# Attention maxima transposed at the fourth place of a head step instead of the fifth, with the sign and the split into two parts moved behind the transpose

## The reference

```
x = x + Wo(softmax(mask(rope(Q) rope(K)^T / sqrt(32))) V) + bo      # Q, K, V from layernorm(x)
x = x + down(silu(gate(ln(x)) * gs) * (up(ln(x)) * us)) * ds        # 512 -> 1408 -> 512
```

## Time and profile before

| | |
|---|---|
| median of 3 runs | 755.08 us (752.31 to 756.74) |
| profiled execution: time, span | 756.7 us, 754.9 us |
| granted TensorE clock, mean | 0.995 |
| busy share of the span: PE, PEld, DVE, ACT, POOL | 97%, 71%, 59%, 41%, 33% |
| stage B, two consecutive steps | about 18.3 us, 14 such pairs with everything in them |

### The profile page before, as it was taken

How to read it: one execution, slowest core, us unless ns; L and a number is a source line. 1 busy time by engine, 2 the same in 40 slices (tenths; PEclk the granted TensorE clock), 3 DMA queues, 4 the chain that set the end, 5 groups by cost and what they waited for, 6 DMA issues and landing times.

```text
span 754.9 us, 10665 instructions
## 1 busy us (share of the span) xinstructions
PE 732.0 (97%) x3563; PEld 537.5 (71%) x3563; DVE 442.2 (59%) x1103; ACT 308.7 (41%) x641; POOL 246.4 (33%) x224
## 2 busy tenths in 40 slices
PE   7999999979999999999999999999999999999996
PEld 7788888755665655555555547878788888888884
DVE  6979584987777777777777637863243125114113
ACT  3232232256666666666655562223322232222221
POOL 0626251502114142414141436832232223223222
PEclk9999999999999999999999999999999999999998
DMA  8586568635566666666676475650001001001001
GB/s 281 187 280 232 197 251 278 251 127 158 167 168 180 166 177 181 170 180 175 167 194 167 111 208 171 250 227 1 0 3 55 0 1 56 0 0 56 1 1 58
DMA packets 54318, 104.39 MB, mean 138 GB/s; under 512 B 14820, under 2 KB 18404, under 8 KB 53748
## 3 DMA queue, kind: packets, MB, share of 16 engines
q1 hardware_dynamic: 54264, 103.72, 44.7%
HBM read 69.62 MB, written 38.21 MB: 143 GB/s over the span
## 4 chain that ended last, share of the span: by engine, by line
PE 83%; issue 5%; DVE 4%; DMA 3%; ACT 2%; POOL 2%; SPq 0%; DVEq 0%; POOLq 0%; ACTq 0%
PE ps L1101 38%; PE ps L1240 17%; PE ps L1316 9%; PE ps L1219 8%; PE ps L1126 8%; DMA q_st<-neg_max_T 2%; PE ps L1093 2%; POOL hid_lo L592 1%; ACT p L680 1%; ACT o_raw L687 1%; PE ps L1137 1%; PE ps L1160 1%; SPq L421 0%; DMA x_st<-in_x 0%; DVE stats L796 0%
## 5 line engine op out<-in xcount | busy, mean ns | idle before, releaser
L680 ACT ACTIVATE p<-ps 128x384 f32<-128x384 f32 (+3 forms) x384 | 159.5, 489 | 35.0 <-PE ps L1219 34.4
L841 DVE CUSTOM_DVE_ANT_0 masked<-ps,mask_qk 128x512 bf16<-128x512 f32 (+1 forms) x240 | 113.6, 502 | 66.9 <-PE ps L1126 66.0
L1219 PE MATMUL ps<-q_st,k_st 99*128 99x384 f32 (+2 forms) x384 | 135.6, 361 | 4.2 <-ACT p L680 1.3
L1240 PE MATMUL ps<-p,v_slot 128*64 128x512 f32 (+3 forms) x768 | 137.3, 494 | 0.2 <-ACT o_raw L687 0.2
L1052 DVE SCALAR_TENSOR_TENSOR hid<-ps,us_sb,silu 128x512 f32<-128x512 f32 x44 | 33.0, 751 | 165.2 <-PE ps L1101 159.5
L1126 PE MATMUL ps<-k_st,q_st 96*128 96x512 f32 (+2 forms) x384 | 127.8, 355 | 1.0 <-DVE row_max L841 0.9
L592 POOL TENSOR_TENSOR hid_lo<-hid,hid_hi 128x512 fp32r<-128x512 f32 x44 | 56.8, 1292 | 172.2 <-ACT hid_hi L756 172.2
L561 POOL TENSOR_SCALAR_AFFINE_SELECT p<-p 128x512 f32<-128x512 f32 x64 | 40.7, 637 | 202.9 <-ACT p L680 202.8
L1240 PEld LDWEIGHTS ps<-p,v_slot 128*64 128x64 f32 x768 | 50.1, 136 | 74.3 <-issue 62.0
L1126 PEld LDWEIGHTS ps<-k_st,q_st 96*128 96x128 f32 x384 | 72.5, 190 | 26.4 <-issue 17.7
L1219 PEld LDWEIGHTS ps<-q_st,k_st 99*128 99x128 f32 x384 | 72.3, 190 | 18.7 <-ACT p L680 9.6
(11 more groups left out here) (119 smaller groups left out, 1081.9 us busy)
## 6 DMA issues: line engine op xcount, KB each, us to landing
qk_scratch<-st_hi SPq DMA_DIRECT2D x32, 512.0 KB, 3.8
q_st<-qk_scratch SPq DMA_DIRECT2D x32, 384.0 KB, 3.9
k_st<-qk_scratch SPq DMA_DIRECT2D x32, 384.0 KB, 5.0
flag_st<-in_ffn SPq DMA_DIRECT2D x32, 264.0 KB, 2.8
ffn_copy<-in_ffn SPq DMA_DIRECT2D x32, 264.0 KB, 3.2
qk_scratch<-st_lo SPq DMA_DIRECT2D x16, 512.0 KB, 3.8
o_T<-o_raw SPq DMA_DIRECT2D x32, 128.0 KB, 4.6
rec_l<-rec_rows SPq DMA_DIRECT2D x32, 128.0 KB, 3.3
```

Of the source, the lines that this page charges most:

```text
L680: act.activation(p32[:, at:at + q0 + w - keep], ps[:, ST_BANK + i % ST_RING, keep - q0:w], ACT.Exp, scale=SCALE).then_inc(exp_done, 1)
L841: ins = dve.tensor_tensor_reduce((masked_a if u < 2 else masked)[:, s_before(i) % 2, col:col + kept], scores, mask_qk[:, 512 - kept:512], ...
L1219: pe.matmul(ps[:, ST_BANK + i % ST_RING, 0:w], k_st[0:K_ALL, slot, kt * P:(kt + 1) * P], q_st[0:K_ALL, slot, q0:q0 + w], start=True, stop= ...
L1240: ins = pe.matmul(ps[VW * a:VW * (a + 1), o_bank(u, half), q0 - 512 * half:512], v_slot[:, slot, kt, :], p32[:, at:at + n], start=(kt == 0 ...
```

## The change

T is moved to place 3, ahead of that place's group of V products, and the S piece that stood there goes to place 4, behind them. What is transposed is `max8` itself, 8 columns and not 16, so T needs line 851 alone. ScalarE then writes the negated high part from PSUM, behind its exponential of place 2. VectorE, behind place 2's piece, waits for that and takes the low part from PSUM. The two DMAs read two tiles of 8 partitions instead of the halves of one. T's bank is now bank 3, so that S(7) waits for it, and S(8) waits for S(4)'s maximum.

```diff
-M_ENTRY = 4
-M_AFTER = 3
+M_ENTRY = 3
+M_AFTER = 2
...
-                for part in range(2):
+                for part, rows in enumerate((neg_hi_T, neg_lo_T)):
...
+                def max_high(u):
+                    act.wait_ge(max_T_ps, u + 1)
+                    act.activation(neg_hi_T[:, u % 2, :], ps[0:KT, M_BANK, 0:P], ACT.Copy, scale=-1.0).then_inc(max_hi, 1)
...
             def next_max(t):
-                act.wait_ge(max_T_ps, t + 2)
                 if t >= 1:
                     act.wait_ge(max_in[(t - 1) % SLOTS], 32 * ((t - 1) // SLOTS + 1))
-                act.copy(neg_max_T[:, (t + 1) % 2, :], ps[0:2 * KT, M_BANK, 0:P]).then_inc(max_T, 1)
+                max_high(t + 1)
...
-            def negate_max(u, step):
...
+            def whole_max(u):
+                dve.wait_ge(s_max, NS * (u + 1))
+                if u > 0:
+                    dve.wait_ge(max_T_ps, u)
+                dve.tensor_reduce(max8[:, :], row_max[:, u % 2, :, :], AX_X, ALU.max).then_inc(max_ready, 1)
+
+            def max_low(u):
+                dve.wait_ge(max_hi, u + 1)
+                dve.scalar_tensor_tensor(out=neg_lo_T[:, u % 2, :], in0=ps[0:KT, M_BANK, 0:P], scalar=-1.0,
+                                         in1=neg_hi_T[:, u % 2, :].bitcast(F32), op0=ALU.mult, op1=ALU.subtract).then_inc(max_T, 1)
...
-                    if t < HEADS - 1 and i < 3:
-                        negate_max(t + 1, i)
+                    if t < HEADS - 1 and i == 0:
+                        whole_max(t + 1)
+                    if t < HEADS - 1 and i == M_ENTRY:
+                        max_low(t + 1)
...
             def transpose_max(v):
                 pe.wait_ge(max_ready, v + 1)
-                if v + 1 < HEADS:
-                    pe.wait_ge(s_max, NS * (v + 1) + s_before(M_ENTRY - S_RING) + 1)
                 if v > 0:
                     pe.wait_ge(max_T, v)
-                pe.transpose(ps[0:2 * KT, M_BANK, 0:P], neg_max[:, :].bitcast(F32), ident[:, :]).then_inc(max_T_ps, 1)
+                pe.transpose(ps[0:KT, M_BANK, 0:P], max8[:, :], ident[:, :]).then_inc(max_T_ps, 1)
```

More of the change, by code:

```diff
@@ L141, in transformer_block @@
         max8 = sb("max8", [P, KT], F32)
-        neg_max = sb("neg_max", [P, 2 * KT], F32R)
-        neg_max_T = sb("neg_max_T", [2 * KT, 2, P], F32)
+        neg_hi_T = sb("neg_hi_T", [KT, 2, P], F32R)
+        neg_lo_T = sb("neg_lo_T", [KT, 2, P], F32R)
         l_cols = sb("l_cols", [P, 4, KT], F32)
@@ L264, in transformer_block @@
         s_max = sem("s_max")
-        max_step = sem("max_step")
         max_ready = sem("max_ready")
         max_T_ps = sem("max_T_ps")
+        max_hi = sem("max_hi")
         max_T = sem("max_T")
@@ L419, in load_max @@
                 slot = u % SLOTS
-                for part in range(2):
-                    sp.dma_start(q_st[K_DOT + part:K_DOT + part + 1, slot, :].bitcast(F32), neg_max_T[part * KT:(part + 1) * KT, u % 2, :]).then_inc(max_in[slot], 16)
+                for part, rows in enumerate((neg_hi_T, neg_lo_T)):
+                    sp.dma_start(q_st[K_DOT + part:K_DOT + part + 1, slot, :].bitcast(F32), rows[:, u % 2, :].bitcast(F32)).then_inc(max_in[slot], 16)
             def move_pair(u):
@@ L672, in _ @@
                         if j == 2:
-                            act.wait_ge(max_T_ps, 1)
-                            act.copy(neg_max_T[:, 0, :], ps[0:2 * KT, M_BANK, 0:P]).then_inc(max_T, 1)
+                            max_high(0)
             def exp_piece(t, i):
@@ L865, in early @@
                     max_piece(u, i)
-                    if u == 1 and i < 3:
-                        negate_max(0, i)
+                    if u == 1 and i == 0:
+                        whole_max(0)
+                    if u == 1 and i == M_ENTRY:
+                        max_low(0)
             dve.memset(flag_bits[:, :], 0).then_inc(flag_init, 1)
```

## The result

| | before | changed |
|---|---|---|
| median of 18 runs each, us | 755.1 | 757.91 |
| lowest, highest | 752.31, 759.83 | 755.93, 763.03 |
| ratio | | 1.0044, 95% interval 1.0024 to 1.0064 |
| profiled execution: span, us | 754.9 | 754.4 |

The change costs 0.44%, 3.3 us by the ratio (1.8 to 4.8), 2.8 by the medians. The two spans don't show it: in the changed kernel's profiled execution stage A, which the change doesn't touch, happened to be 3.4 us shorter. Its first products ran at a granted clock of 1.00 (10 to 15 us), those of the kernel before at 0.67, which is some 1.6 us; and the trace before has a DVE product (line 825) of 3.44 us instead of 1.20, behind which TensorE waited 0.9 at 30 us. So only the same stretch of the two traces can be compared. Stage B, from its first V product to its last group, takes 278.8 us (168.94 to 447.77) and took 274.3 (173.10 to 447.39), so 4.5 more.

The account below looks back on a forecast made before the run. PE's order was taken as the bound, busy 18.16 of 18.30 us in two steps of stage B. The terms summed to +4.8 us, added to the median 755.08: 759.9 us, forecast 756 to 764, range 753.3 to 765.5.

Parts of the forecast that it names:

- T at its new place: Stage B, place 3: T, almost free behind V products, costs 0.10 more in each of 28 steps, +2.8 us.
- the wait for the whole maximum: PE at place 3: T waits for line 851, 0.16 in 22 steps and 0.25 in six, +5.0 us.
- S(9) held by the moved piece: Behind the V group: DVE takes S(4) ahead of S(5)'s maximum, holding S(9) by 0.20 in 28 steps, +5.6 us.
- relief on ACT, even steps: Stage B, even steps: the output copy no longer waits for T, ending a 0.40 stall in 14 steps, -5.6 us.
- the transfer's stalls: PE's five waits for the maxima's transfer, 2.5 us in all, end because both parts are ready earlier, -2.0 us.
- start of stage B: Where stage B begins: T no longer waits for line 859, the next S piece comes 0.8 earlier, -0.7 us in all.
- end: Last steps, bound by ACT: they lose one copy ahead of the output's, -0.3 us.
- The signs: Expected in stage B's trace: two steps 0.35 to 0.5 longer, even S(5) to S(9) about 1.6, no transfer waits.
- S(9) unheld: Rival, behind the V group: DVE reaches S(5)'s maximum 0.2 earlier, the 5.6 vanishes, 754.3 us; chance 0.20.
- S(8) was not held: Rival: S(8) held too, or the relief fails, +0.1 to +0.4 in each second step, 762 to 766; chance 0.15.
- The transfer did come earlier: Rival: rows come no earlier because SyncE's queue or the transfers ahead set their landing, 761.9 us; chance 0.06.
- load a table: Rival, ScalarE: the negating copy loads a function table, two loads in each of 31 steps, about 835 us; chance 0.01.

Follow-up runs that it names:

- experiment 5: Changed kernel with T transposing 8 constant identity columns, not waiting for the whole maximum: ratio to before 0.9990, 4.1 us less than the changed kernel.
- experiment 4: Changed kernel with the 512-column score piece of place 4 exchanged for place 8's 384-column one: ratio to before 0.9997, 3.5 us less than the changed kernel.
- experiment 1: Changed kernel's new flow (ScalarE negates, VectorE takes the low part from PSUM) with T at old place 4, behind the V products: ratio to before 1.0012.
- experiment 6: Kernel before with only ScalarE's order changed in even steps (output half's copy, exponential of place 4, then maxima): ratio 0.9972, 2.1 us less.
- experiment 8: Changed kernel with the V group behind place 2, narrow piece at place 4, output half copied first in even steps: ratio to before 1.0309, 23 us slower.
- experiment 2: Kernel before, its old flow (VectorE negates and splits, then T) kept, with T moved to place 3: ratio 1.1059, +80 us.
- experiment 3: Changed kernel with T behind ST(3), directly ahead of the V group: ratio to before 1.0021, 1.7 us less than the changed kernel.
- experiment 9: Changed kernel with T transposing constant identity columns and standing behind ST(3), directly ahead of the V group: ratio to before 1.0033.

## Why the prediction was right, and where it was off

It forecast +4.8 us and 759.9; +3.3 and 757.9 were measured, inside the range. Slower by over 0.5% had the highest chance (0.59); the ratio stands at 0.44%, just inside "same", with an interval across that bound. By its steps, sizes from the two traces:

| term | forecast | found | shown by |
|---|---|---|---|
| T at its new place, and the wait for the whole maximum | +2.8, +5.0 | +7.9 together | 0.87 and 0.77 against 0.74 ahead of the group, 0.52 against 0.29 behind it; of this the wait alone 4.5 (experiment 5) |
| S(9) held by the moved piece | +5.6 | +4.2 | S(5) to V group 1.87 against 1.73; experiment 4 |
| relief on ACT, even steps | -5.6 | -5.5 | experiments 1, 6 |
| the transfer's stalls | -2.0 | -1.8 | no such wait left |
| start of stage B | -0.7 | -0.8 | first V product 0.8 earlier against the S pieces of `EARLY` |
| end | -0.3 | -0.3 | last whole pair 15.58 against 15.88 |
| sum | +4.8 | +3.7 | stage B 4.5 longer and 0.8 earlier; runs: +3.3 (1.8 to 4.8) |

**The place and the wait.** Right in mechanism and sum. T waits 0.16 and 0.25, to the hundredth, though the longer wait came in eight steps, not six; what delays DVE in steps 9 and 16 is not shown. That TensorE pays for the wait was right: taking the dependency away gave 4.1 us back on the chip. It is worth 4.5 rather than 5.0: T starts 0.25 and 0.16 late, the V group only 0.22 and 0.14. The rest, 3.4, is the place itself: T is nearly free behind V products and costs 0.13 between score products. The estimate of 0.11 from the Trainium skill, "TensorE: Matmul & The Clock Gate", section "LDWEIGHTS (loading the stationary operand)", is near the 0.13 that experiment 5 shows (0.64 less 0.51), and 0.056 is not.

**S(9)** was the mis-sized term, by 1.4 us the largest miss of the sum: 0.15 a step, not 0.20. DVE took S(4) 0.61 behind its start, not 0.64, and released S(9) at 1.96, not 1.98, behind the group; the wait is real, and a narrower piece removes it.

**The relief** was right. S(5) to the V group in even steps fell from 2.12 (249.52 to 251.64) to 1.88 (265.85 to 267.73), which is 0.39 less, and 0.15 more for S(9). But half of it did not need T's move: it comes from ScalarE's order alone.

**The signs.** Two steps take 18.77 and more, 0.44 to 0.59 above 18.33, where 0.35 to 0.5 was named; the forecast's own terms give 0.56 a pair. S(5) to S(9) in even steps fell to 1.45 (265.85 to 267.30), not 1.6. No wait of ST(7) for ACT and none for the transfer was left, as named.

**Rivals.** S(9) unheld (754.3) is nearly what experiment 4 built (it still takes 0.17), and gave 0.9997. S(8) was not held in the steady steps. The transfer did come earlier. The flow does not load a table: the negating copy ran 32 times at 252 ns between exponentials. The rule of the Trainium skill, "ScalarE: Activation LUTs", section "Table sets: the hidden batching unit", that copy is in every set, so holds here for the copy with a scale too.

**What the prediction lacked.** It gave DVE's wait for ACT's copy the price nothing, with the idle time behind it as cover. That held here; experiments 1 and 8 show how near the edge it is: the cover is gone as soon as T stands behind the V group.

## What to carry to other kernels

In a stream that one engine works through in order, price a moved instruction by the distance from start to start at both places, not by its duration: here the same transpose was nearly free behind V products and cost 0.13 us between score products, and the piece that took its old place inherited the loss it used to hide. When work is moved ahead of a long group, look at what then stands first behind the group: its consumer has run dry by then, and a wide piece there delays what waits for the second piece. And before moving the producer to relieve a consumer's queue, try to reorder that queue: ScalarE's order alone gave 0.28% where the move lost 0.44%.

## What the runs showed of the hardware

- A DVE instruction on 8 columns lasted 2.16 us instead of 0.17 beside a GpSimd product of two tensors of 1024 columns, and ended with it (experiment 2, six times). In the changed kernel the weights' test beside the same product takes 1.93 instead of 0.69, where idle time hides it.
- After TensorE had stood for 4 us the granted clock was 0.58 on average over the next 5 us, with 16 V instructions at 4.39 us instead of 2.38; after waits of 0.25 it stayed at 1.00. In experiment 2 three V groups also ran slowly behind a wait of 1.5 to 1.6 (the one at 211 us 3.85 instead of 2.15, at a granted clock of 0.64 from 212 to 216); behind the other waits of that length the V groups took their usual time.
- A transpose directly ahead of V products cost 0.10 us more than one place earlier (ST(2) to the V group 0.73 to 0.76 in experiments 3 and 9, 0.64 in experiment 5), with constants as with the maxima.
